# Stacks of attention layers: two matmuls put ahead of the transpositions, and one addition ahead of the splitting of the norms

## The reference, cut to what matters

```
for i in range(6):
    x = attn_layer(shift_tokens(x), Wqkv[i], q_scale[i], k_scale[i], Wo[i]) + x
    x = ffn_layer(shift_tokens(x), ...) + x

attn_layer: q, k, v = split(x @ Wqkv)           # 16 heads of 64
            q = l2norm(q) * qs;  k = l2norm(k) * ksc;  rotary on both
            windows of 32 tokens: softmax(8 q k^T + mask) v over this window and the one before
            out @ Wo
ffn_layer:  layer norm, then (a * gelu(gate)) @ W2 + b2, with a, gate = split(xn @ W1 + b1)
```

## Time and profile before

| | |
|---|---|
| median of 3 runs | 4420.13 us (4412.47 to 4425.89) |
| the profiled execution, its own time | 4411.89 us |
| span of its trace | 4410.1 us |
| first stack, first to last q projection | 393 to 2175 us |
| second stack | 2554 to 4335 us |
| busy in the span: TensorE, VectorE, ScalarE, GpSimd | 4119.1, 3484.4, 3076.0, 1802.7 us |

### The profile page before, as it was taken

How to read it: one execution, slowest core, us unless ns; L and a number is a source line. 1 busy time by engine, 2 the same in 40 slices (tenths; PEclk the granted TensorE clock), 3 DMA queues, 4 the chain that set the end, 5 groups by cost and what they waited for, 6 DMA issues and landing times. The chain is left out here.

```text
span 4410.1 us, 111762 instructions
## 1 busy us (share of the span) xinstructions
PE 4119.1 (93%) x43089; PEld 2408.1 (55%) x43089; DVE 3484.4 (79%) x4981; ACT 3076.0 (70%) x7032; POOL 1802.7 (41%) x1071
## 2 busy tenths in 40 slices
PE   7997999999999999999967589999999999999998
PEld 3443555555555555555536445555555555555554
DVE  5775888888888888888735478888888888888886
ACT  3555777777777777777762267777777777777776
POOL 3112444444444444444404534444444444444442
PEclk7999999999999999999986699999999999999999
DMA  2213444444443444444300044434434444444342
GB/s 43 30 21 80 100 107 97 102 103 94 106 107 84 109 103 99 101 103 99 74 10 3 3 119 102 106 90 110 105 87 108 101 104 94 100 102 106 90 97 54
DMA packets 232516, 380.72 MB, mean 86 GB/s; under 512 B 59364, under 2 KB 122336, under 8 KB 231688
## 3 DMA queue, kind: packets, MB, share of 16 engines
q1 hardware_dynamic: 231560, 372.20, 36.3%
q10 hardware_dynamic: 384, 0.79, 0.1%
HBM read 39.22 MB, written 1.05 MB: 9 GB/s over the span
## 5 line engine op out<-in xcount | busy, mean ns | idle before, releaser
L835 POOL TENSOR_TENSOR b_prob<-b_prob,b_rinv 128x768 f32<-128x768 f32 x384 | 564.9, 1471 | 1857.9 <-DVE b_rinv L1262 1857.9
L841 POOL TENSOR_TENSOR b_prc<-b_prc,b_sws 128x1024 f32<-128x1024 f32 x384 | 910.8, 2372 | 64.3 <-DMA b_sws<-b_prs 64.1
L1130 ACT ACTIVATE b_prob<-ps,b_nmx 128x96 f32<-128x96 f32 x3072 | 751.2, 363 | 0.0
L879 PEld LDWEIGHTS ps<-ident,b_prob 128*128 128x128 f32 x3072 | 377.5, 141 | 421.7 <-issue 302.4
L1203 DVE SCALAR_TENSOR_TENSOR b_prc<-ps,b_qks,b_rot 128x512 f32<-128x512 f32 x768 | 571.2, 744 | 10.6 <-ACT b_sq L1091 10.2
L1205 DVE SCALAR_TENSOR_TENSOR b_prs<-ps,b_qks,b_rot 128x512 f32<-128x512 f32 x768 | 570.3, 743 | 0.0
L1243 DVE TENSOR_TENSOR b_prc<-b_prc,ps 128x512 f32<-128x512 f32 x384 | 264.2, 688 | 381.7 <-PE ps L937 307.4
L1216 DVE SCALAR_TENSOR_TENSOR b_rsp<-b_rhi,b_minus_hi,b_rn 128x512 fp32r<-128x512 f32 x192 | 412.3, 2147 | 110.6 <-ACT b_rn L1077 110.6
L879 PE MATMUL ps<-ident,b_prob 128*128 128x128 f32 x3072 | 464.8, 274 | 5.3 <-ACT b_pT L1066 5.3
L1111 ACT ACTIVATE b_oT<-ps 128x512 f32<-128x512 f32 x384 | 227.0, 591 | 341.9 <-PE ps L895 341.9
L1066 ACT ACTIVATE b_pT<-ps 128x512 f32<-128x512 f32 x724 | 435.6, 602 | 15.1 <-PE ps L879 10.9
(11 more groups left out here) (292 smaller groups left out, 7295.7 us busy)
## 6 DMA issues: line engine op xcount, KB each, us to landing
b_sws<-b_prs SPq DMA_DIRECT2D x1536, 128.0 KB, 2.3
b_vs<-b_va SPq DMA_DIRECT2D x384, 256.0 KB, 3.8
b_wqkv<-in_L_ffn_Wqkv SPq DMA_DIRECT2D x96, 192.0 KB, 3.6
b_xs<-y SPq DMA_DIRECT2D x126, 128.0 KB, 2.5
b_wo<-in_L_ffn_Wo SPq DMA_DIRECT2D x96, 64.0 KB, 3.1
b_xs<-y SPq DMA_DIRECT2D x42, 127.8 KB, 2.3
b_rot<-in_rot SPq DMA_DIRECT2D x2, 2048.0 KB, 7.8
b_w<-in_L_ffn_W SPq DMA_DIRECT2D x24, 170.5 KB
```

Of the source, the lines that this page charges most:

```text
L835: pool.tensor_tensor(prob[:, r, :, P - KEYS:P], prob[:, r, :, P - KEYS:P], rinv[:, r % 2, :].rearrange("p (b a) -> p b a", a=1).broadcast_ ...
L841: pool.tensor_tensor(prc[:, r, :, :], prc[:, r, :, :], sws[:, r % 2, :, :], ALU.add)\
L879: t = pe.transpose(bank[6][:, i * P:(i + 1) * P], prob[:, kd, 4 * e + 2 * h + m, :], ident[:, :])
L1130: g = act.activation(prob[:, kb, i, P - KEYS:P], wide[0][:, e * CH + m * KEYS:e * CH + (m + 1) * KEYS], ACT.Exp, bias=nmx[:, kb % 2, i:i + 1])
```

## The change

On TensorE the spreads come directly behind the q projection, ahead of turn 0, and the first mask comes ahead of turn 1 instead of behind it; slots with `before == 5` keep turn 0 and turn 1 where they were. On VectorE, in even slots in which feed-forward work follows (positions 0, 4, 6, 8, 10, 12 and 14 of the half layers that have it), the y add is issued ahead of the split; position 2 keeps the old order. No instruction is added or removed.

```diff
+                def mask(kb, e, pe=pe):
+                    pe.matmul(wide[0][:, e * CH:e * CH + 4 * KEYS], identb[:, :], band[:, 1 if kb % 2 else 0, :],
+                              start=True, stop=False, skip_group_check=True)
...
                     if d:
                         UD, kd = um(d)
+                    if d and before == 5:
                         turn(UD, kd, 0)
                     if b:
...
                         pe.matmul(bank[3][:, :], take[:, 2 * (kb % 2) + 1, :], rsp[:, :], start=True, stop=True)\
                             .then_inc(S["nb_mm"], 1)
+                    if d and before != 5:
+                        turn(UD, kd, 0)
                     key_bank_free(f0)
...
-                    if d:
+                    if d and before == 5:
                         turn(UD, kd, 1)
                     if b:
                         pe.wait_ge(S["exp_done"], ONE + UB)
-                        for e in range(2):
-                            if e:
-                                pe.wait_ge(S["kn_done"], ONE + UB + 1)
-                            pe.matmul(wide[0][:, e * CH:e * CH + 4 * KEYS], identb[:, :], band[:, 1 if kb % 2 else 0, :],
-                                      start=True, stop=False, skip_group_check=True)
+                        mask(kb, 0)
+                    if d and before != 5:
+                        turn(UD, kd, 1)
+                    if b:
+                        pe.wait_ge(S["kn_done"], ONE + UB + 1)
+                        mask(kb, 1)
...
-                    if b and j % 2 == 0:
+                    follows = before in (0, 2, 4) or ok is not None
+                    if b and j % 2 == 0 and not follows:
                         n = twos(b)
                         dve.wait_ge(S["rn_done"], ONE + n + 1)
                         dve.scalar_tensor_tensor(out=rsp[:, :], ...).then_inc(S["split_done"], 1)
...
                         dve.tensor_tensor(ys, bank[3][:, :], ys, ALU.add).then_inc(S["y_add"], 1)
+                    if b and j % 2 == 0 and follows:
+                        n = twos(b)
+                        dve.wait_ge(S["rn_done"], ONE + n + 1)
+                        dve.scalar_tensor_tensor(out=rsp[:, :], ...).then_inc(S["split_done"], 1)
```

More of the change, by code:

```diff
@@ L1222, in slot @@
                         dve.tensor_tensor(ys, bank[3][:, :], ys, ALU.add).then_inc(S["y_add"], 1)
+                    if b and j % 2 == 0 and follows:
+                        n = twos(b)
+                        dve.wait_ge(S["rn_done"], ONE + n + 1)
+                        dve.scalar_tensor_tensor(out=rsp[:, :], in0=rhi[:, :].bitcast(F32), scalar=minus_hi[:, 0:1], in1=rn[:, :],
+                                                 op0=ALU.mult, op1=ALU.add).then_inc(S["split_done"], 1)
                     if before == 0:
```

## The result

The changed kernel takes 4376.4 us (median of 4 runs, 4370.9 to 4380.3), the kernel before 4423.0 (4 runs): a ratio of 0.9896, with a 95% interval of 0.988 to 0.9913, so 38 to 53 us less. The forecast of 53 us less was at the upper edge of what was measured; its time of 4367 us is 9 us low.

A forecast was written before the change was run, and what follows sets the result against it. TensorE, busy 98% inside a stack, was taken to bound the kernel, with a hidden mask wait. Gains of 21 + 1 + 10 + 10 + 0 + 11 = 53 us took 4420 to 4367 us, range 4340 to 4402.

The forecast's parts named there:

- The bound and the hidden wait: TensorE sets the pace; second mask's wait for VectorE's L1245 costs 0.16 us a slot, 21 us at positions 6-8, 12-14.
- Turn 1's slack of 0.16: On TensorE, turn 1 can start at 2.62, after ScalarE's copy of turn 0, and is due at 2.78.
- rival 1: ScalarE's copy ends 0.16 or more later, so a new wait replaces the old: about 4395 us; chance 0.17.
- a sign of being wrong: Turn 1 waiting for ScalarE's copy in most slots; first spread waiting for the split at positions other than 2.
- Positions 4 and 10: Variance matmul L1008 starts 0.47 us earlier at position 4, 0.44 at position 10: 10 us each.
- The y add costs the split nothing: On VectorE, GpSimd's L841 sets the split's end, so a y add of 0.68 us in front costs 0.
- Positions 0 to 3 and the first 19 slots: Position 2: 0, bounds ±0.35 us a slot; positions 0, 1, 3: 11 us less; slots without feed-forward work: 0.
- Rival 2: VectorE isn't released earlier at positions 4 and 10: 20 us less gain, about 4387 us; chance 0.10.
- Rival 3: TensorE weight loads come uncovered, 0.10 us a time; two such places cost 67 us, ending at 4434; chance 0.04.
- the four new neighbours: New TensorE successions: q to spread, spread to transposition, transposition to k, mask to transposition; one uncovered load costs 34 us.
- Rival 4: Second mask's load is paid even without a wait, 0.10 us a slot: 13 us less gain, 4380; chance 0.03.

The follow-up runs named there:

- Experiment 2: Two kernels: changed kernel with both masks kept behind turn 1, 0.9924 of the kernel before; changed kernel with spreads kept behind turn 0, 0.9987.
- the TensorE part alone: TensorE's new order, with VectorE keeping split before y add everywhere, against the kernel before: ratio 0.9956, 11 to 27 us less.
- the VectorE part alone: The changed code of VectorE with TensorE's old order, against the kernel before: ratio 0.9991, no difference that can be told.

## Why the prediction was right

**The bound and the hidden wait**: shown. The 0.16 us came to 21.8 us at positions 6 to 8 and 12 to 14 (forecast 21), disappeared with the spreads put back, and came back for 0.12 at even and about 0.08 at odd positions in the old order when the wait was cut down to 96 columns.

**Turn 1's slack of 0.16** (rival 1): right in place and size. Experiment 2 takes the slack away, and the wait for the copy appears, at 0.04 us a slot, because copy and due time fall together. In the list of waits of the changed kernel turn 1 waits for the copy 339 times, which I had named as a sign of being wrong; the list counts loads issued early, and the distance from the mask to turn 1 (0.16) shows that it cost nothing.

**Positions 4 and 10**: 9.7 us at position 10 (10 forecast), and as forecast it needs both parts. 8.1 and 6.7 at position 4 (10 forecast), for two reasons. In most slots (13 of 22) L1257 started at 1.70 to 1.73, not at the forecast 1.63: the split ended at 0.82, and only then did the first spread's load start (0.87), uncovered, which I had left out of the sum. That the first spread waits for the split away from position 2 I had named as a sign of being wrong, and at position 4 it is one, for about 0.1 us a slot:

```profile
1012.36 0.19 PEld L939 LDWEIGHTS ps<-b_rsp,b_take 128*128 128x128 f32 x1 [0.67 <-DVE b_rsp L1235]
```

In five other slots the split ended later still (0.98 to 1.46), and L1257 followed.

**The y add costs the split nothing**: true where I used it, not in general. I read from the earlier trace rows that the split's end is set by L841's end. That holds only for a split that starts behind L841. One that starts first takes 0.74 us, as in the row of 843.87, and it is then L841 that takes longer, 2.49 instead of 2.35. That is what the Trainium skill says, page "SBUF — State Buffer", section "SBUF: two separate sides": whichever started first keeps the pair. I had cited the rule and used half of it. Position 2 in the experiment with the y add always first is its other half, 12 us. The blocked one doesn't lose the whole of the overlap: this L841 overlapped the split by 0.27 us and lasted 0.14 longer.

**Positions 0 to 3 and the first 19 slots**: the terms that were off. Positions 0, 1 and 3 gave 11.9 and 12.7 (11 forecast, "mostly the mask"). At position 1 that is so: the TensorE part alone gives the whole 4.8. At position 0 the number came out by luck: the full change gives 3.1 (3.7 forecast), but the TensorE part alone loses 1.4 there and the VectorE part alone gives 5.2, so what gains is the y add ahead of the split, and the earlier spreads seem to take part of it back. Position 2 was put at 0 and cost 3.3 and 0.2. In its slots in which L841 goes first the forecast weighed 0.44 - 0.16 against a split 0.2 to 0.3 earlier; the slot became 0.25 longer (median 8.27 before, 8.52 after) and the split ended only 0.03 earlier (1.67 and 1.64), so that last term was too large. In the others the length follows the end of L841, which in the slots shown waited for the swap's DMA: 2.20 to 3.86 us into the slot in one profile, 2.20 to 3.03 in the next. The first 19 slots were put at 0 and cost 3.2 and 11.5; why was not looked into. Position 2, the first 19 slots and position 4 make the stacks gain 47 instead of 53, and with the 9 us outside the stacks that gives the 38 of the profiled span.

**Rival 2** was wrong for the change as made and is what the TensorE part alone shows. **Rival 3** (uncovered loads): none of the four new neighbours costs anything; the distances are those of the forecast to 0.01 us. **Rival 4**, the rule of the Trainium skill (page "TensorE: Matmul & The Clock Gate", Part 3, section "The mechanism") that a load overlaps only with matmuls of another row group: in the changed kernel turn 1, whose first load lasts 0.14 us, starts 0.16 us behind the mask. Where the two masks follow each other without a wait, the second, whose load lasts 0.10, starts 0.16 behind the first too (and experiment 2). So these loads were not paid, and the trace disagrees with that rule for loads of the whole array; the same section also speaks of a background weight buffer, for which a load is pulled ahead, and with that the trace agrees. From the second mask to the scores, which use another tile size, it is 0.25 us; the 0.09 more are there in every kernel and their cause was not looked into.

## What to carry to other kernels

On an engine whose matmul records overlap, a busy share of 98% can hide a wait in every iteration: compare the distance between the same two starts in many iterations, and look for an iteration where the releaser was early. Before moving an instruction past a wait, write down all that the waiting instruction needs with its times. Where an instruction is held by two things that end together, moving one of them gains nothing, and a wait with another gate just behind it is worth nothing to remove. Where two engines hold each other up, an instruction put ahead is free while the other engine runs anyway, and costs time when without it one could have started before the other engine.

## What the runs showed of the hardware

The split and L841 hold each other up in whichever order they start. In the kernel before, 178 of 192 splits started while an L841 was running, and all of them ended 0.55 us behind its end, so that they lasted up to 2.87 us; in 13 the split was first and lasted 0.74 (but for one that started with L841 and lasted 2.90), and there L841 took 2.81 us in the median instead of 2.35. With the y add ahead of it in most even slots the split's median fell from 2.35 us (192 of them) to 1.11 (154 of them at the new place), and VectorE's busy time from 3484 to 3362 us. That by itself is worth no time: in the VectorE part alone it fell to 3368.5 as well. The busy time had counted the waiting for L841.

A weight load that waits for a semaphore costs time beyond the wait, because it no longer runs beneath the matmul before it: 0.05 us where the semaphore came exactly on time (turn 1 with the masks not moved), 0.1 us for W1 at position 5 and for the first spread at position 4.

Why the strips start later behind the cut mask than the scores do, which is the difference between odd and even positions there, was not looked into further.
